# A four-layer attention stack: float32 keys and queries in layer 0, maxima moved ahead of the first eight-head phase, and an end in parts

## Chip, cores and metric

The kernel runs on one core of a Trainium2 chip, as one program written instruction by instruction for each engine, with semaphores between them. The metric is the device time of one execution in microseconds; the value quoted is the median of several runs. TensorE is PE below, VectorE is DVE, ScalarE is ACT, GpSimd is POOL, and SP is the engine that here only issues DMA transfers.

## What is computed

The input x has 4 images of 256 channels by 1024 positions, all in float32. Four self-attention layers follow each other:

```
layer 0: q = Wq x + bq (32 rows), k = Wk x + bk (32 rows), v = Wv x + bv (256 rows)
         out = gamma * (v softmax(q'k)') + x, then a batch norm over all images
layer 1: group norm, q, k, v of 256 rows, one head, output projection, x + out
layer 2: group norm (xn), eight heads of 32 rows, output projection, xn + out
layer 3: group norm, eight heads of 32 rows, output projection, x + out
```

## The kernel before

**Precision.** Most products use a fast 32-bit format of PE that keeps fewer bits. Where the full precision matters an operand is split into a high part (the value rounded to the fast format) and a low part (the rest, rounded again), and three products are added: high x high, low x high, high x low. A plain float32 matmul is also possible; the trace shows each as two records.

**Layers 0 and 1** (`one_head`) go image by image, b = 0 to 3. An image has eight tiles i of 128 queries. For each tile PE makes the scores of 128 x 1024 in one of the two slots of psD, DVE takes the row maximum, ACT the exponential, POOL multiplies by the inverse sum, PE transposes into psA, ACT and DVE split the result into PTH and PTL, and PE weighs the values into psO. The list `order` says which unit (scores "s", keys and queries "k", values "v") gets the next slot; a unit may have its slot only when the unit two places ahead has been taken. In layer 0 `project` makes keys and queries together, 64 rows: 12 matmuls from WH, WL, XH and XL. ACT writes the high part into KL (`high`), DVE the low part into QL (`low`), and SP copies them with six transfers (L736) into the stacks KH and QH of 96 rows, which the scores read with one product. All of this for the next image stands at tile 5 of the current one. At the start w0 is loaded, then image 0, then the constants; DVE splits w0 into WH and WL, ACT and DVE split X.

**Layers 2 and 3** (`eight_heads`) are one stream of 16 phases, for each a group of four heads of one image. A phase has 64 steps: half h, tile j and head q. A step is one score matmul (L1031, 97 rows: 96 of the stacks KS and QS and one that subtracts the maximum) and one exponential (L1209) into PR, which has room for four tiles j. POOL adds the tiles up into PA, `ADDS` = 5 additions a half (L1250); the weighted sum is on PE (`weigh`, L927), and `sums` (L939) adds PA and the last two tiles over the partitions. Between the steps stand side units, placed by hand by step number and made in four banks of psD in turn: "k", "q" and "K", "Q" (keys and queries of this group and of the next, six matmuls each half), "v" values, "m" and "a" (one maximum each of 128 x 512 scores, L1000 on PE and L1082 on DVE, for half 0 and half 1), "T" and "t" (the transposes that make the row of maxima, MROW), "z" (`sums`), and "p" (one 128 x 512 block of the output projection and its residual, L1073). "t" also carries the group means, on which POOL's factors and then ACT's normalised input (`XN_AT`, step 31) wait. Twelve (`EARLY`) of the 32 maxima for half 1 stand at the end of the phase before, the other 20 in the phase itself.

Ahead of phase 0 stands a fill (`phase(None, ...)`, place 0) with only side units. Its keys and queries are rounded on ACT, POOL makes the low parts (`low`, L1234), and SP copies them into the stack (24 transfers, L1281 and L1283). Then come 32 "m" and 12 "a" with "T" between, and "K", "Q" of group 1 behind the first maxima; ACT may take K only when the stack of group 0 has landed, since it overwrites SL. SP issues stack(0), stack(1) and then the row of maxima, L1288:

```python
FIRST_AT = {"k": (0.1, 0.2), "q": (0.3, 0.4), "b": (1,), "K": (8, 10), "Q": (12, 14)}
...
stack(0)
stack(1)
maxima(0, 0)
```

The tail, after phase 15, holds the last two pieces of `weigh`, `sums` of the last half, DVE's scaling (`take_half`), four output blocks with residuals, and one transfer of the last image.

Of the kernel before, what the change touches and what calls it, by code (L numbers as in the profile page):

```python
# [5 lines left out]
ALU = mybir.AluOpType  # L6
# [32 lines left out]
def attention_stack(nc, x, w0, w1, w2, w3, wp1, wp2, wp3, wv1, par_d, ident_d, gmat_d, out):  # L39
    with ExitStack() as ctx:  # L40
# [90 lines left out]
        def single_heads():  # L131

            with ExitStack() as stage:
# [14 lines left out]
                GBV = sb("GBV", [PART, CT], F32, stage)  # L148
                BNF = sb("BNF", [PART, CT, 2], F32, stage)
# [13 lines left out]

                s_const, s_memset = sem("constants_loaded"), sem("memsets_done")
# [5 lines left out]
                def one_head(layer):  # L170
# [43 lines left out]
                    with nc.Block() as block:  # L214
                        @block.tensor
                        def _(e):
# [9 lines left out]

                            def project(i, b):
                                if i == 0:
# [4 lines left out]
                                width = PART if L1 else 2 * K0  # L233
                                cols = slice(PART * i, PART * i + width)
                                for k, (ww, xx) in enumerate(((WH, XH), (WL, XH), (WH, XL))):
                                    if i == 0 and k == 2:
                                        e.wait_ge(xl_done, CT * (b + 1))
                                    for h in range(2):
                                        mv = slice(h * HALF, (h + 1) * HALF)
                                        for t in range(CT):  # L240
                                            mm = e.matmul(psD[0:width, slot, mv], ww[:, t, cols], xx[:, t, mv],
# [87 lines left out]
                            for b in range(B):  # L329
                                more = b + 1 < B  # L330
                                for i in range(NT):
# [3 lines left out]
                                    if not L1 and i == 5 and more:  # L335
# [24 lines left out]
                        def _(e):  # L360
# [145 lines left out]
                            for b in range(B):  # L506
                                more = b + 1 < B
                                for i in range(NT):
# [23 lines left out]
                                    if more and i == 5:  # L532
# [13 lines left out]
                        def _(e):  # L546
# [63 lines left out]
                            for b in range(B):  # L610
                                more = b + 1 < B
                                for i in range(NT):
# [8 lines left out]
                                    if more and i == 5:  # L621
# [11 lines left out]
                        def _(e):  # L633
# [7 lines left out]
                            def shift(b):  # L641
                                for t in range(CT):
# [123 lines left out]
        FIRST_AT = {"k": (0.1, 0.2), "q": (0.3, 0.4), "b": (1,), "K": (8, 10), "Q": (12, 14)}  # L766
        W3_AT = 28
        BANKS = 4
        SCORE_BANKS = 3

        def side_units(g, first=False, last=False):

            early, late = (0 if last else EARLY), (0 if first and g == 0 else 2 * ROWS - EARLY)
            tiles = ([("late", a) for a in range(2 * ROWS - late, 2 * ROWS)]
                     + [("first", a) for a in range(0 if last else 2 * ROWS)] + [("late", a) for a in range(early)])
# [3 lines left out]
            else:  # L779
                halves, step = dict({} if last else SIDE_AT[g]), STEPS / (4 * ROWS)  # L780
# [4 lines left out]
            units = [(u, at, i) for u, at_halves in halves.items() for i, at in enumerate(at_halves)]  # L785
            if first and g:
                units = [x for x in units if x[0] != "z" or x[2] == 0]
            for (kind, a), at in zip(tiles, ats):
                units.append(("a" if kind == "late" else "m", at, a))
                if a == 2 * ROWS - 1:  # L790
                    units.append(("t" if kind == "late" else "T", at + (LAG + 0.01) * step, 0))
# [25 lines left out]
        assert all(x[0] in "amtTzp" for u in UNITS[:4] for x in u[-BANKS:])  # L817
# [51 lines left out]
        def eight_heads_in(stage):  # L869
# [43 lines left out]
            with nc.Block() as block:  # L913
                @block.tensor
                def _(e):
# [15 lines left out]
                    def sums(full, P, h):  # L931

                        for j in (NT, *range(NT - DIRECT, NT)):
                            if j == NT:
                                wait(e, sum_done, ADDS * (2 * P + h + 1))
# [7 lines left out]
                            elif j < NT - 1:  # L943
# [22 lines left out]
                    def unit(place, r, k, P, p, G, g, norm, layers):  # L966
# [28 lines left out]
                        elif u in "am":  # L995
                            q, tile, h = i // NT, i // 2 % (NT // 2), i % 2
                            group = p if u == "a" and place and i >= EARLY else g
                            if u == "m" and i % NT == 0:
                                stacks_filled(e, G, [q])
                            mm = e.matmul(full, QS[0:STACK, group, int(u == "a"), q, tile * PART:(tile + 1) * PART],  # L1000
# [375 lines left out]
```

## Time and profile before

| what | us |
|---|---|
| median of 3 runs (lowest to highest) | 1654.55 (1653.58 to 1658.74) |
| the profiled execution's own time | 1656.73 |
| its span | 1654.8 |
| PE busy | 1542.6 (93%) |
| DVE, ACT, POOL busy | 1036.7, 866.1, 988.2 |
| first scores of layer 0 | 22.86 |
| first score of phase 0 | 581.86 |

The span is cut where the work changes: layers 0 and 1 up to 521 us, the fill up to 581.7, the 16 phases of some 65 us each up to 1628.6, and the tail. Times in the rows are microseconds from the start of the span; a busy share says how long an engine had work in flight, not that it was at its peak.

### The profile page before, as it was taken

The numbers are of one execution on the slowest core, as the hardware profiler recorded it, in microseconds if no ns is written. First come the engines' busy times: TensorE is split into PE (matmuls) and PEld (weight loads), VectorE is DVE, ScalarE is ACT, GpSimd is POOL, SyncE is SP. The second block draws the span as 40 slices with busy tenths as digits, with TensorE's granted clock in tenths as the row PEclk, the third lists the DMA queues.
The fourth block names the chain that finished last, engine by engine and source line by source line (L and its number), as shares of the span: only waits on it lengthen the run. The fifth ranks groups of instructions, "written<-read, shape, count | busy, mean of one in ns | idle before, by whom it ended". The sixth has DMA issues, their size and how long they took to land.

```text
span 1654.8 us, 21821 instructions
## 1 busy us (share of the span) xinstructions
PE 1542.6 (93%) x8238; PEld 993.2 (60%) x8238; DVE 1036.7 (63%) x1652; ACT 866.1 (52%) x1441; POOL 988.2 (60%) x392
## 2 busy tenths in 40 slices
PE   3888879999997789999999999999999999999986
PEld 2777757888886455555555555455555555555532
DVE  3556554544542666776776777677777777677741
ACT  3444324433433156657657567556665664765752
POOL 1212121221214168798698798967878879779874
PEclk7999989999999699999999999999999999999998
DMA  4000000000000501230330321303303123033000
GB/s 164 20 20 1 20 1 0 1 1 0 20 1 21 137 10 25 53 77 1 77 77 2 77 49 49 77 1 77 74 5 77 42 62 77 7 96 78 27 1 25
DMA packets 31720, 67.46 MB, mean 41 GB/s; under 512 B 7488, under 2 KB 9600, under 8 KB 31616
## 3 DMA queue, kind: packets, MB, share of 16 engines
q1 hardware_dynamic: 31616, 66.08, 16.2%
q8 instruction: 65, 1.06, 0.3%
q14 instruction: 39, 0.32, 0.1%
HBM read 8.08 MB, written 4.19 MB: 7 GB/s over the span
## 4 chain that ended last, share of the span: by engine, by line
PE 53%; POOL 7%; DVE 3%; SPq 2%; ACT 1%; issue 1%; POOLq 0%; DMA 0%; DVEq 0%; ACTq 0%
PE psO L927 12%; PE psD L1000 11%; PE psD L89 11%; PE psA L1031 9%; POOL PA L1250 6%; PE psD L939 5%; PE psO L1031 4%; DVE BNS L1082 2%; SPq L1281 1%; ACT PR L1209 1%; SPq L1283 1%; POOL SL L1234 1%; DVE sums_turned L1061 0%; DMA QS<-SL 0%; POOLq L913 0%
## 5 line engine op out<-in xcount | busy, mean ns | idle before, releaser
L1082 DVE TENSOR_REDUCE BNS<-psD 128x1 f32<-128x512 f32 x1024 | 638.0, 682 | 225.8 <-PE psD L1000 225.7
L1250 POOL TENSOR_TENSOR PA<-PA,PR 128x2048 f32<-128x2048 f32 x128 | 587.3, 4589 | 34.1 <-ACT PR L1209 18.9
L1209 ACT ACTIVATE PR<-psA 128x512 f32<-128x512 f32 x688 | 392.2, 604 | 242.5 <-PE psA L1031 218.2
L1000 PE MATMUL psD<-KS,QS 96*128 96x512 f32 x1024 | 417.2, 413 | 21.3 <-DMA QS<-SL 10.7
L1031 PE MATMUL psA<-QS,KS 97*128 97x512 f32 x688 | 290.9, 425 | 3.9 <-DMA QS<-MROW 2.2
L1209 ACT ACTIVATE PR<-psO 128x512 f32<-128x512 f32 x336 | 202.4, 602 | 160.2 <-PE psO L1031 160.2
L650 POOL TENSOR_SCALAR P<-P,RS 128x1024 f32<-128x1024 f32 x64 | 71.7, 1122 | 347.5 <-DVE RS L389 347.5
L927 PE MATMUL psO<-PR,V 128*32 128x512 f32 x2048 | 249.5, 605 | 7.5 <-DVE A L1067 5.6
L1000 PEld LDWEIGHTS psD<-KS,QS 96*128 96x128 f32 x1024 | 198.6, 194 | 76.1 <-DVE BNS L1082 17.8
L1250 POOL TENSOR_TENSOR PA<-PR 128x2048 f32<-128x2048 f32 x32 | 146.8, 4587 | 119.0 <-ACT PR L1209 119.0
L1031 PEld LDWEIGHTS psA<-QS,KS 97*128 97x128 f32 x688 | 130.9, 191 | 113.1 <-issue 57.9
L1031 PE MATMUL psO<-QS,KS 97*128 97x512 f32 x336 | 146.9, 437 | 0.7 <-ACT PR L1209 0.7
L927 PEld LDWEIGHTS psO<-PR,V 128*32 128x32 f32 x2048 | 53.6, 110 | 130.8 <-issue 82.4
L596 ACT ACTIVATE PTH<-psA 128x1024 fp32r<-128x1024 f32 x64 | 65.5, 1024 | 108.8 <-PE psA L279 108.8
L589 ACT ACTIVATE P<-psD,NM 128x1024 f32<-128x1024 f32 x64 | 71.2, 1112 | 95.3 <-DVE NM L382 95.3
L382 DVE TENSOR_REDUCE NM<-psD 128x1 f32<-128x1024 f32 x64 | 77.6, 1214 | 65.6 <-PE psD L89 65.5
L1031 PEld LDWEIGHTS psO<-QS,KS 97*128 97x128 f32 x336 | 63.7, 190 | 83.7 <-issue 46.5
L294 PE MATMUL psO<-PTH,VH 128*128 128x512 f32 x256 | 106.5, 416 | 4.4 <-issue 3.2
L395 DVE TENSOR_TENSOR PTL<-psA,PTH 128x1024 fp32r<-128x1024 f32 x64 | 78.2, 1222 | 39.7 <-ACT PTH L596 39.5
L294 PE MATMUL psO<-PTL,VH 128*128 128x512 f32 x256 | 102.2, 399 | 0.0
L294 PE MATMUL psO<-PTH,VL 128*128 128x512 f32 x256 | 102.2, 399 | 0.0
L1234 POOL TENSOR_TENSOR SL<-SL,SH 128x1024 fp32r<-128x1024 f32 x34 | 80.3, 2382 | 36.4 <-ACT SH L1159 36.4
(145 smaller groups left out, 1937.9 us busy)
## 6 DMA issues: line engine op xcount, KB each, us to landing
KS<-SH SPq DMA_DIRECT2D x128, 128.0 KB, 2.3
QS<-SH SPq DMA_DIRECT2D x128, 128.0 KB, 2.4
KS<-SL SPq DMA_DIRECT2D x64, 128.0 KB, 2.4
QS<-SL SPq DMA_DIRECT2D x64, 128.0 KB, 2.4
X<-x SPq DMA_DIRECT2D x4, 1024.0 KB, 7.5
out<-X SPq DMA_DIRECT2D x4, 1024.0 KB, 4.3
XN<-w SPq DMA_DIRECT2D x2, 768.0 KB, 8.0
KH<-KL SPq DMA_DIRECT2D x8, 128.0 KB, 2.3
```

The source lines that it names most:

```text
L89: last = e.matmul(out_ap, w, m, start=(i == 0), stop=(i == len(terms) - 1))
L294: mm = e.matmul(psO[:, t, :], vv[:, s, cols], pp[:, h, s, :], start=(s == k == 0), stop=(s == NT - 1 and k == 2))
L382: e.tensor_reduce(NM[:, g % 4:g % 4 + 1], psD[:, index[u] % 2, :], AX.X, ALU.max, negate=True).then_inc(max_done, 1)
L395: e.tensor_tensor(PTL[:, i // 4, :, cols], psT.rearrange("p (s t) -> p s t", s=NT), PTH[:, i // 4, :, cols].bitcast(F32), ALU.subtract).th ...
L927: mm = e.matmul(psO[cols, 0, :], V[:, j, PART * p + CH * q:PART * p + CH * q + CH], source[:, q, :], start=(j == 0), stop=(j == NT - 1))
L939: mm = e.matmul(full[CH * q:CH * q + CH, :], ones[:, 0:CH], source[:, q, :], start=(j == NT), stop=(j == NT - 1))
L1000: mm = e.matmul(full, QS[0:STACK, group, int(u == "a"), q, tile * PART:(tile + 1) * PART], KS[0:STACK, group, q, h * HALF:(h + 1) * HALF], ...
L1031: e.matmul(score_bank(s, p), KS[0:STACK + 1, p, q, j * PART:(j + 1) * PART], QS[0:STACK + 1, p, h, q, :], start=True, stop=True).then_inc( ...
L1082: top = e.tensor_reduce(MXH[:, h, q, tile:tile + 1], full, AX.X, ALU.max)
L1209: e.activation(PR[:, J % 4, (s % QUADH) * HALF:(s % QUADH + 1) * HALF], score_bank(s, p), ACT.Exp, scale=scale).then_inc(exp_done, 1)
L1234: e.tensor_tensor(SL[:, which, :].bitcast(F32R), SL[:, which, :], SH[:, which, :], ALU.subtract).then_inc(low_done, 1)
L1250: e.tensor_tensor(PA[:, :], PR[:, (J - 1) % 4, :] if j == 1 else PA[:, :], PR[:, J % 4, :], ALU.add).then_inc(sum_done, 1)
```

## The change

Layer 0: a tile WKQ gets the 64 columns of w0 for keys and queries by a transfer of its own, ahead of image 0 and w0; `project_narrow` multiplies it with X in plain float32 (two matmuls for each half of the positions); the projection of the next image with its `high` and `low` stands at tile 1 instead of 5; the values now wait for the split parts; POOL's `shift` of X waits until the projection has read X.

Eight heads: the fill makes only the 32 "m"; the 12 "a" move into phase 0, which so has 76 maxima over its 64 steps; K and Q of group 1 stand behind 23 maxima; DVE makes the low parts of group 0; SP sends the row ahead of stack(1). ("e" is the new name of the early maxima.)

End: in the last half POOL makes three additions, and `sums` reads PA and four tiles; the two output blocks of half 0 stand at steps 44 and 48 of the last phase and are stored from there; the other two stay in the tail, each with a transfer of its own.

```diff
+                wkq_loaded = sem("wkq_loaded")
...
-                            if i == 5 and b + 1 < B:
+                            if i == (5 if L1 else 1) and b + 1 < B:
                                 order += [("k", k, b + 1) for k in range(min(2, NQK))]
...
+                            def project_narrow(b):
+                                if b == 0:
+                                    e.wait_ge(wkq_loaded, 16)
+                                e.wait_ge(x_loaded[b], 16)
+                                slot = slot_taken(("k", 0, b))
+                                for h in range(2):
+                                    mv = slice(h * HALF, (h + 1) * HALF)
+                                    mm = split_products(e, psD[0:2 * K0, slot, mv],
+                                                        [(WKQ[:, t, :], X[:, b, t, mv]) for t in range(CT)])
+                                mm.then_inc(unit_full, 1)
...
                             def values(i, b):
                                 slot = slot_taken(("v", i, b))
+                                if not L1 and i == 0:
+                                    if b == 0:
+                                        e.wait_ge(w_low[layer], 1)
+                                    e.wait_ge(xh_done, CT * (b + 1))
+                                    e.wait_ge(xl_done, CT * (b + 1))
...
-                                    if not L1 and i == 5 and more:
+                                    if not L1 and i == 1 and more:
                                         project(0, b + 1)
...
-                                    if more and i == 5:
+                                    if more and i == (5 if L1 else 1):
                                         for k in range(min(2, NQK)):
                                             low(k, b + 1)
...
-                                    if more and i == 5:
+                                    if more and i == (5 if L1 else 1):
                                         for k in range(min(2, NQK)):
                                             high(k, b + 1)
...
                             def shift(b):
+                                e.wait_ge(unit_full, index["k", 0, b] + 1)
...
+                            e.dma_start(WKQ[:, :, :], w_dram[0][:, :, 0:2 * K0]).then_inc(wkq_loaded, 16)
+                            e.dma_start(X[:, 0], x_v[:, 0]).then_inc(x_loaded[0], 16)
                             e.dma_start(raw(0), w_dram[0]).then_inc(w_loaded[0], 16)
-                            e.dma_start(X[:, 0], x_v[:, 0]).then_inc(x_loaded[0], 16)
...
-        FIRST_AT = {"k": (0.1, 0.2), "q": (0.3, 0.4), "b": (1,), "K": (8, 10), "Q": (12, 14)}
+        FIRST_AT = {"k": (0.1, 0.2), "q": (0.3, 0.4), "b": (1,), "K": (28.1, 30.1), "Q": (32.1, 34.1)}
+        LAST_AT = {"p": (43.5, 47.5)}
+        LAST_ADDS = NT - 5
...
-            early, late = (0 if last else EARLY), (0 if first and g == 0 else 2 * ROWS - EARLY)
+            early = 0 if last or first and g == 0 else EARLY
+            late = 0 if first and g == 0 else 2 * ROWS if first else 2 * ROWS - EARLY
...
-                halves, step = dict({} if last else SIDE_AT[g]), STEPS / (4 * ROWS)
+                halves, step = dict(LAST_AT if last else SIDE_AT[g]), STEPS / max(len(tiles), 4 * ROWS)
...
-                        for j in (NT, *range(NT - DIRECT, NT)):
+                        for j in (NT, *range(adds + 1, NT)):
...
-                            mm = output(full, i, 2 * P, layers[3])
+                            mm = output(full, i, 2 * P + (G is None), layers[3])
...
-                        sums(bank(4, AFTER), NGRP - 1, 1).then_inc(d_full, 1)
-                        for i in range(2 * CT):
-                            e.wait_ge(vec_free, TAIL["vector"] + AFTER + i - BANKS + 2)
-                            output(bank(4, AFTER + 1 + i), i, 2 * NGRP, 3).then_inc(d_full, 1)
+                        sums(bank(4, AFTER), NGRP - 1, 1, LAST_ADDS).then_inc(d_full, 1)
+                        for c in range(CT):
+                            e.wait_ge(vec_free, TAIL["vector"] + AFTER + c - BANKS + 2)
+                            output(bank(4, AFTER + 1 + c), 2 * c + 1, 2 * NGRP, 3).then_inc(d_full, 1)
...
+                        if P is None:
+                            events += [(5, which, 0, "low") for which in range(2)]
+                        for _, which, k, what in sorted(events):
+                            if what == "low":
+                                e.wait_ge(high_done, which + 1)
+                                e.tensor_tensor(SL[:, which, :].bitcast(F32R), SL[:, which, :], SH[:, which, :],
+                                                ALU.subtract).then_inc(low_done, 1)
...
-                            for which in range(4):
-                                low(which // 2, which % 2)
+                            for which in range(2):
+                                low(1, which)
...
-                            for j in range(1, ADDS + 1):
+                            for j in range(1, (LAST_ADDS if G is None and h else ADDS) + 1):
...
                     stack(0)
+                    maxima(0, 0)
                     stack(1)
-                    maxima(0, 0)
...
-                    e.wait_ge(vec_free, TAIL["vector"] + AFTER + 1 + 2 * CT)
-                    e.dma_start(out_v[:, B - 1], X[:, B - 1]).then_inc(s_out, 16)
-                    e.wait_ge(s_out, 16 * B)
+                    e.wait_ge(vec_free, units_taken(NGRP, "p"))
+                    e.dma_start(out_v[:, B - 1, :, 0:HALF], X[:, B - 1, :, 0:HALF]).then_inc(s_out, 16)
+                    for c in range(CT):
+                        e.wait_ge(vec_free, TAIL["vector"] + AFTER + 2 + c)
+                        e.dma_start(out_v[:, B - 1, c, HALF:N], X[:, B - 1, c, HALF:N]).then_inc(s_out, 16)
+                    e.wait_ge(s_out, 16 * (B + CT))
```

## Rows read from the trace of the kernel before

**Rows 1.** The page: the chain that ended last, shares by engine.

```profile
PE 53%; POOL 7%; DVE 3%; SPq 2%; ACT 1%; issue 1%; POOLq 0%; DMA 0%; DVEq 0%; ACTq 0%
```

**Rows 2.** Stretches: busy time (instructions) per engine, PE's granted clock, DMA share, GB/s.

```profile
core 0: us, PE busy (x) PEld busy (x) DVE busy (x) ACT busy (x) POOL busy (x), PEclk, DMA share, GB/s
66.00:72.00 6.00, 4.00 (x15) 3.47 (x16) 1.39 (x2) 1.87 (x3) 0.37 (x1) 0.72 0.20 46
547.00:553.00 6.00, 0.37 (x2) 0.00 (x0) 0.00 (x0) 0.25 (x1) 0.00 (x0) 0.73 0.75 173
566.00:574.00 8.00, 7.84 (x15) 3.64 (x14) 7.93 (x15) 0.00 (x0) 0.00 (x0) 0.50 0.82 190
845.00:910.00 65.00, 64.87 (x365) 37.97 (x363) 46.26 (x80) 40.95 (x71) 55.90 (x25) 1.00 0.22 50
```

**Rows 3.** Timeline of the start: start, duration, engine, line, idle before and its releaser.

```profile
7.23 0.23 DVE L493 TENSOR_SCALAR GBV<-PAR 128x2 f32<-128x2 f32 x1 [2.05 <-DMA group_mean<-gmat]
10.16 1.94 PE L241 MATMUL psD<-XH,WH 128*64 128x512 f32 x4 [10.16 <-ACT XH L557]
14.84 1.11 ACT L576 ACTIVATE KL<-psD,PAR 64x1024 fp32r<-64x1024 f32 x1 [4.82 <-PE psD L241]
```

**Rows 4.** The chain: start, duration; one output block in a steady phase.

```profile
726.92 1.72 PE psD L89 x4
```

**Rows 5.** Timeline, images 1 to 2 of layer 0: tile 5 to the new scores.

```profile
108.75 1.14 PE L241 MATMUL psD<-XH,WH 128*64 128x512 f32 x4 [0.84 <-ACT XH L557]
...
111.26 1.21 DVE L395 TENSOR_TENSOR PTL<-psA,PTH 128x1024 fp32r<-128x1024 f32 x1
...
114.33 1.03 PE L279 MATMUL psA<-identity,P 128*128 128x128 f32 x8
...
120.49 0.70 PE L89 MATMUL psD<-KH,QH 96*128 96x512 f32 x2 [2.38 <-DMA QH<-QL]
```

**Rows 6.** Timeline: transposes of tile 2 in image 0, of tile 1 in image 1.

```profile
36.89 1.94 PE L279 MATMUL psA<-identity,P 128*128 128x128 f32 x8 [1.61 <-DVE PTL L395]
```

```profile
80.98 1.07 PE L279 MATMUL psA<-identity,P 128*128 128x128 f32 x8 [1.98 <-DVE PTL L395]
```

**Rows 7.** The chain through the fill ahead of phase 0.

```profile
550.30 2.34 DMA QS<-SL
...
557.46 1.38 PE psD L89 x6
...
559.12 13.25 DVE BNS L1082 x22
...
579.82 1.90 DMA QS<-MROW
```

**Rows 8.** Timeline: the first maximum of the fill.

```profile
540.99 1.19 PE L1000 MATMUL psD<-KS,QS 96*128 96x512 f32 x2 [10.70 <-DMA QS<-SL]
```

**Rows 9.** Groups by shape: count, busy us, mean ns of a subtraction of 128x1024.

```profile
L1234 POOL TENSOR_TENSOR SL<-SL,SH 128x1024 fp32r<-128x1024 f32 x34 | 80.3, 2382 | 36.4 <-ACT SH L1159 36.4
...
L427 DVE TENSOR_TENSOR XL<-X,XH 128x1024 fp32r<-128x1024 f32 x8 | 9.4, 1222 | 4.8 <-ACT XH L557 4.8
```

**Rows 10.** Timeline: ACT at step 31 of phase 0.

```profile
617.51 0.60 ACT L1209 ACTIVATE PR<-psA 128x512 f32<-128x512 f32 x1 [3.00 <-POOL SC L129]
```

**Rows 11.** The chain: a weighing of sixteen records, then the tail.

```profile
1571.37 1.85 PE psO L927 x16
...
1627.99 4.54 POOLq L913
...
1632.66 5.38 PE psD L939 x24
```

**Rows 12.** Timeline: the second residual of the tail.

```profile
1646.19 0.75 DVE L1073 SCALAR_TENSOR_TENSOR X<-psD,PAR,X 128x512 f32<-128x512 f32 x1 [2.04 <-PE psD L89]
```

**Rows 13.** The page: DMA issues, KB each, median us to landing.

```profile
out<-X SPq DMA_DIRECT2D x4, 1024.0 KB, 4.3
...
WP<-wp SPq DMA_DIRECT2D x2, 256.0 KB, 2.9
```

More of the change, by code:

```diff
@@ L148, in single_heads @@
                 GBV = sb("GBV", [PART, CT], F32, stage)
+                WKQ = sb("WKQ", [PART, CT, 2 * K0], F32, stage)
                 BNF = sb("BNF", [PART, CT, 2], F32, stage)
@@ L771, in side_units @@
         def side_units(g, first=False, last=False):
-            early, late = (0 if last else EARLY), (0 if first and g == 0 else 2 * ROWS - EARLY)
-            tiles = ([("late", a) for a in range(2 * ROWS - late, 2 * ROWS)]
-                     + [("first", a) for a in range(0 if last else 2 * ROWS)] + [("late", a) for a in range(early)])
+            early = 0 if last or first and g == 0 else EARLY
+            late = 0 if first and g == 0 else 2 * ROWS if first else 2 * ROWS - EARLY
+            tiles = ([("a", a) for a in range(2 * ROWS - late, 2 * ROWS)]
+                     + [("m", a) for a in range(0 if last else 2 * ROWS)] + [("e", a) for a in range(early)])
             if first and g == 0:
@@ L784, in side_units @@
                 ats = [(i + 0.5) * step - 1 for i in range(len(tiles))]
-            units = [(u, at, i) for u, at_halves in halves.items() for i, at in enumerate(at_halves)]
+            units = [(u, at, 2 * i if last and u == "p" else i) for u, at_halves in halves.items() for i, at in enumerate(at_halves)]
             if first and g:
@@ L788, in side_units @@
             for (kind, a), at in zip(tiles, ats):
-                units.append(("a" if kind == "late" else "m", at, a))
+                units.append((kind, at, a))
                 if a == 2 * ROWS - 1:
-                    units.append(("t" if kind == "late" else "T", at + (LAG + 0.01) * step, 0))
+                    units.append(("t" if kind == "a" else "T", at + (LAG + 0.01) * step, 0))
             return sorted(units, key=lambda x: x[1])
@@ L816, in attention_stack @@
         assert LOOP["all"] % BANKS == 0
-        assert all(x[0] in "amtTzp" for u in UNITS[:4] for x in u[-BANKS:])
+        assert all(x[0] in "ametTzp" for u in UNITS[:4] for x in u[-BANKS:])
         def base_of(kind, place, r):
@@ L994, in unit @@
                                                         [(WP[layer][:, t, cols], par(f"bv{layer}", 2)[:, t:t + 1]) for t in range(CT)])
-                        elif u in "am":
+                        elif u in "ame":
                             q, tile, h = i // NT, i // 2 % (NT // 2), i % 2
-                            group = p if u == "a" and place and i >= EARLY else g
+                            group = p if u == "a" else g
                             if u == "m" and i % NT == 0:
                                 stacks_filled(e, G, [q])
-                            mm = e.matmul(full, QS[0:STACK, group, int(u == "a"), q, tile * PART:(tile + 1) * PART],
+                            mm = e.matmul(full, QS[0:STACK, group, int(u in "ae"), q, tile * PART:(tile + 1) * PART],
                                           KS[0:STACK, group, q, h * HALF:(h + 1) * HALF], start=True, stop=True)
@@ L1101, in take @@
                         else:
-                            add_residual(i, proj, full, layers[3]).then_inc(vec_free, 1)
+                            add_residual(i, B - 1 if G is None else proj, full, layers[3]).then_inc(vec_free, 1)
                     def phase(P, p, G, g, place, r, layers, proj=None, norm=None, norm_b=None):
@@ L1124, in _ @@
                     take_half(bank(4, AFTER), 1, 1)
-                    for i in range(2 * CT):
-                        e.wait_ge(d_full, TAIL["all"] + AFTER + 2 + i)
-                        add_residual(i, B - 1, bank(4, AFTER + 1 + i), 3).then_inc(vec_free, 1)
+                    for c in range(CT):
+                        e.wait_ge(d_full, TAIL["all"] + AFTER + 2 + c)
+                        add_residual(2 * c + 1, B - 1, bank(4, AFTER + 1 + c), 3).then_inc(vec_free, 1)
                     e.drain()
```

21 lines of the change are left out of this document (11 added, 10 removed).

## The prediction

> **What bounds the kernel now.** I read the page first, then the stretches, then the timeline and the chain at the few places that the diff touches. The chain by engine [rows 1] puts 53% of the span on TensorE (PE) and 7% on GpSimd (POOL); the rest is thin. The stretches [rows 2] show that this average hides two kinds of time. In a steady phase of the eight-head layers (845 to 910 us) PE is busy without a gap at full clock, and the diff changes no instruction there, nor in layer 1. In the fill ahead of phase 0 (547 to 582 us), at the start, at the batch changes of layer 0 and in the tail, PE waits for something else, and its granted clock is partly or wholly at 0.50, the lower level of 1.2 GHz. Every edit sits in one of those places, so I cost them one at a time and let the rest shift as a block.
>
> **1. Start of layer 0.** Before, X is rounded on ACT and the first projection matmul goes at 10.16; the result is taken by ACT at 14.84 [rows 3]. After, PE multiplies X and WKQ as they come. It needs X and the constants, which DVE has at 7.23 [rows 3]. The price is that of float32 matmuls: an output unit of 512 columns (two matmuls, four records) takes 1.72 us at high clock [rows 4], twice that, 3.4, at half the clock. The narrow projection is four such matmuls: 3.4 us high, 6.9 low. The twelve old ones fill 10.16 to 14.8, 0.39 us each, where a batch later four take 1.14 (0.28 each, [rows 5]): this stretch runs low, so I take 6.8. 7.2 + 6.8 = 14.0 against 14.8, **-0.8 us**. Bounds: -4.2 (high clock) to 0. The split of W0 on DVE and XH, XL run beside it and are needed only for the values at tile 3; without that cover they would cost the 3 us that the old order paid. The small WKQ transfer stands ahead of X, w0 behind it; I cost both at nothing.
>
> The Trainium skill, "FP8 and Floating Point Precision", section "TensorE Precision Notes", counts true FP32 as four passes through the array, against three one-pass products in the old form, so it speaks against this edit in PE time. The rows agree: 2 x 1.72 = 3.4 us for the new projection against some 3 x 1.1 for the old. By the rule alone each projection would be a third dearer, by the rows about a tenth; the sum goes by the rows.
>
> **2. Batch changes in layer 0 (three).** Take batch 1 to 2 [rows 5]. The projection begins at 108.75 and fills PE for 3 us, the next transposes go at 114.33, and the first scores at 120.49, after PE stood 2.38 us for the last stack transfer. With projection, high and low part at tile 1, the transposes of tile 6 wait only for PTL of tile 5, done at 111.26 + 1.21 = 112.5: 1.7 us earlier. The weighing and the scores then follow with no wait: another 2.4 us. Together **-4.1 us each**, -12.3 for three; the first change also leaves 6 us at a mean clock of 0.72 [rows 2], worth 1.6. At tile 1 the work comes back. Batch 0: PE idles 1.61 us ahead of the transposes of tile 2 [rows 6], at low clock. A projection of 6.8 us, or about 5 if the clock rises during it, less that idle, with the high and low part behind it on ACT and DVE (queued behind them: the next maximum and PTL, for which the transposes wait): about +3. Batches 1 and 2: the 1.98 us of idle lies ahead of tile 1's transposes [rows 6], and the projection comes behind them, so it covers nothing; some of it at low clock makes it 4.9 us, of which 1.3 is won back because the weighing behind it finds the clock high: +3.6 each. Sum: -12.3 - 1.6 + 3 + 7.2 = -3.7, say **-3.5 us**. Bounds: -12 if all hides, +6 if all three cost 6.8 and the clock gives nothing.
>
> **3. Fill.** Before: K of group 1 stands behind two maxima, and ACT may take it only when the whole first stack has landed (550.30 + 2.34, [rows 7]), so PE works 0.4 of the 6 us from 547 to 553 [rows 2]; then DVE reduces at 13.25/22 = 0.602 us a tile [rows 7], 44 tiles in all; and the row goes out at 579.82, when SP has issued stack(1), and lands 1.90 us later [rows 7]. After:
> - Low parts on DVE: a pass of that size takes 1.22 us there against 2.38 on POOL [rows 9], so they end 2.2 us earlier, and so does all of the first stack.
> - SP issues a head's six transfers every 3.9 us. The first maximum, at 540.99 [rows 8], goes at 538.8. DVE then always has work: eight maxima take 4.9 us. It starts at 539.6, maximum 19 is done at 551.8, and K may be computed; the stack has landed at 550.5.
> - K, Q of group 1: four units of six matmuls, 1.38 us each at high clock [rows 7], up to twice that low; with two maxima between each, PE needs 9.1 us if the first runs low and the clock then rises, and DVE waits some. Maximum 31 is done at about 563.1, the row is made at 564.1, sent at once and lands in some 2 us: phase 0 begins at 566.5 instead of 581.86.
>
> That is **-15.4 us**. Bounds: -18 (K, Q at high clock), -12 (all at low clock). Stack(1) now follows the row on SP: 24 issues from 565.2, landed at 583, 17 us into phase 0; the maxima that read it come at step 27, some 30 us in, so 13 us cover it.
>
> **4. Phase 0** gets twelve more maxima of 0.24 us spacing on PE, 2.8 us. Its 32 maxima of half 1 end at step 26, so their transpose goes at step 29, at about 613.3 in the old timing, behind step 28's weighing. The row lands at about 616.9, where the score of step 32 would want it at 614.4. But ACT stood until 617.51 for the factors anyway, 3.00 us [rows 10], because POOL's five additions end so late; of the late row 0.5 us shows. Queued behind that transpose on PE are the group means, and behind those POOL's factors and ACT's input; the means come just ahead of POOL. Some of the 2.8 hides where POOL leads. **+2 us**; bounds 0 and +4.
>
> **5. Tail.** Before, the last weighing ends at 1628.6; POOL's fifth addition, begun at 1627.99, is awaited to 1632.53; the sums take 5.38 us until 1638.04 [rows 11]; then the half is scaled, four output units and residuals follow, and a transfer of 1 MB closes at 1654.8. After: three additions, done two steps of 4.7 us earlier; the sums read PA and four tiles, forty records, at the pace of the high clock (1.85 us per sixteen, [rows 11]) 4.7 us, since PE comes without a gap. Two output units of 1.72 us are moved into steps 44 and 48, where PE has slack behind POOL's cadence; I let them delay the last weighing by 0.8. So sums end at 1629.4 + 4.7 = 1634.1. From there to the end of the second residual it took 8.9 us (1646.19 + 0.75 less 1638.04, [rows 12]): 1643.0. The last piece is 256 KB, 2.9 us in the row of that size instead of 4.3 [rows 13]. End 1645.9: **-8.9 us**. Bounds: -11 (no delay, high clock in the outputs) to -4 (sums at low clock, +4.7).
>
> **Sum**: -0.8 - 3.5 - 15.4 + 2.0 - 8.9 = -26.6 us. The profiled execution took 1656.73 us for its span of 1654.8, 2.2 us above the median of the three runs; it gives 1630.1, and off the median 1654.55 it gives **1628 us** (-1.6%).
>
> **Rivals.**
> - *High clock.* PE is fed with fewer gaps at the start, at tile 1 and in the fill, and the clock stays high there: -3.4 at the start, -3 in the fill, -4 in layer 0: 1618 us. Against it: at 566 to 574 us the clock was 0.50 although PE worked steadily between maxima [rows 2]. Chance 0.17. Beside it stands the Trainium skill, "TensorE: Matmul & The Clock Gate", section "What's actually happening": the throttled state is the default and activity releases it. By that rule denser work would bring this case; the trace so far shows both.
> - *Fill won, phase 0 loses.* Stack(1) or the row of half 1 comes late after all and phase 0 stretches; of -15.4 + 2 only about -2 stays: 1640 us. It needs 13 us of slack to be wrong, or DVE to fall behind, which is busy 46 of 65 us in a phase [rows 2] and gets 8 more. Chance 0.12.
> - *Tail does little*: the moved units delay exponentials and the sums run at low clock: -3 instead of -8.9: 1634 us. Chance 0.12.
> - *Slower.* The moved projection holds one of two score slots until DVE has the low part. If each time everything queues up in series (6.8 projection, 1.1 high, 1.3 low, 1.2 maximum, 1.1 exponential, 1.1 normalisation: 12.6 us) layer 0 loses 3 x 12.6 - 13.9 = 24 us and eats the rest, -22; from 14 us each the kernel is slower than no change can explain, 1660 us. Against it: score 4 and the exponential of tile 3 don't wait for it. Chance 0.02.
> - *Nothing*: the waits named are plainly on the chain, so no net effect has 0.01.
>
> The forecast itself (1622 to 1634) has 0.56. A measurement here tells 0.3%, 5 us, from no change. Cases below 1649.6 hold 0.97; within, 0.01; slower, 0.02. The range takes in the forecast, most of the high-clock case and the phase 0 case: 1617 to 1640.
>
> **What would show it.** No wait for the stack transfer at the batch changes, a gap at tile 1 instead; phase 0's first score at about 562 instead of 581.86, with what layer 0 gave; ACT still waiting for POOL's factors at step 31; two additions fewer in the tail, and sums of about 4.7 us right behind the last weighing. The prediction is wrong if DVE idles over 5 us within the fill's maxima, if phase 0 takes over 72 us, or if layer 0 ends later than before.

## Result and the profile after

The changed kernel took 1629.39 us (median of 4 runs, 1626.74 to 1632.45) against 1654.07 us for the kernel before on the same chip: a ratio of 0.9845 with a 95% interval of 0.9820 to 0.9871, about 25.7 us or 1.5% faster. The forecast was 1628. Its profiled execution was the slowest of the four, 1632.45 us with a span of 1630.7; it is 24.3 us below the profiled execution of before. Executions of one kernel differ by 5 to 11 us here, more than most of the parts below are worth; what the parts share is told apart in the traces.

The page after, the chain by engine. PE's share rose from 53 to 55% and POOL's fell from 7 to 5% [rows 1].

```profile
PE 55%; POOL 5%; DVE 3%; SPq 2%; ACT 1%; issue 1%; DMA 1%; DVEq 0%; ACTq 0%; POOLq 0%
```

**The start.** Timeline of the changed kernel, to be read beside [rows 3].

```profile
6.64 1.28 ACT L576 ACT_TABLE_LOAD   x1 [6.64 <-DMA X<-x]
...
8.02 5.04 PE L89 MATMUL psD<-X,WKQ 128*64 128x512 f32 x8 [8.02 <-DMA group_mean<-gmat]
...
13.09 1.11 ACT L595 ACTIVATE KL<-psD,PAR 64x1024 fp32r<-64x1024 f32 x1 [3.09 <-PE psD L89]
...
18.73 0.60 SPq L757 DMA_DIRECT2D QH<-QL  x1
...
21.96 2.08 PE L89 MATMUL psD<-KH,QH 96*128 96x512 f32 x4 [8.90 <-DMA QH<-QL]
```

PE waits for the constants, the last of the small transfers, which now land 0.8 us later than the 7.23 of [rows 3]. The eight records take 5.04 us, between the two prices of the prediction (the weight loads of the first records are 0.85 us apart, those of the last 0.43). ACT has the result 1.75 us earlier than before, but the last stack transfer, issued at 18.73, is read only at 21.96, 3.2 us later, where each was 2.3 us on the page before; with the first scores at 22.86 before, 0.9 us is left.

**A batch change and what the projection costs at tile 1.** Timeline of the changed kernel: images 0 to 1, then tile 1 of image 1.

```profile
66.27 0.63 PE L89 MATMUL psD<-KH,QH 96*128 96x512 f32 x2
```

```profile
77.99 1.06 PE L298 MATMUL psA<-identity,P 128*128 128x128 f32 x8 [1.99 <-DVE PTL L414]
...
78.98 5.34 PE L89 MATMUL psD<-X,WKQ 128*64 128x512 f32 x8
...
84.37 1.11 ACT L595 ACTIVATE KL<-psD,PAR 64x1024 fp32r<-64x1024 f32 x1 [3.15 <-PE psD L89]
...
85.51 1.27 DVE L386 SCALAR_TENSOR_TENSOR QL<-psD,PAR,KL 64x1024 fp32r<-64x1024 f32 x1 [4.14 <-ACT KL L595]
...
87.58 1.04 PE L298 MATMUL psA<-identity,P 128*128 128x128 f32 x8
```

No scores wait for a transfer any more ([rows 5] had 2.38 us). But transposes to transposes now take 9.6 us (77.99 to 87.58) at tile 1, where they took 5.7 before (80.98 to 86.70): the wait of 1.99 us still stands ahead of the projection [rows 6], and the projection behind it. At the end of the image 4.3 us are won (1.7 behind tile 5 and 2.6 behind tile 6), so an image is only 0.4 us shorter.

**The fill.** The chain of the changed kernel, to be read beside [rows 7].

```profile
529.90 2.34 DVE SL L1138 x2
...
535.51 2.35 DMA QS<-SL
537.86 0.14 issue
537.99 13.10 PE psD L1024 x23
551.10 2.67 PE psD L89 x6
553.77 0.47 PE psD L1024 x2
554.24 1.38 PE psD L89 x6
...
562.52 1.81 DMA QS<-MROW
564.33 0.14 issue
564.46 0.76 PE psA L1055
```

This is the order that the prediction laid out: 23 maxima without a break from 538.0, the first K unit at low clock (2.67 us), the next at 1.38, and the row sent when it is made. Phase 0 starts at 564.46 instead of 581.86. Counted from the last residual of layer 1 (521.59 before, 520.98 after) the fill shrank from 60.3 to 43.5 us.

**Phase 0.** Timeline and stretches of the changed kernel; the columns of the second are those of [rows 2]. The last line of the timeline is the first score of phase 1.

```profile
597.48 0.55 SPq L1318 DMA_DIRECT2D QS<-MROW  x1
...
600.88 0.60 ACT L1239 ACTIVATE PR<-psA 128x512 f32<-128x512 f32 x1 [2.74 <-POOL SC L129]
...
610.93 0.50 PE L1024 MATMUL psD<-KS,QS 96*128 96x512 f32 x1 [0.99 <-DVE BNS L1106]
...
612.22 3.28 PE L951 MATMUL psO<-PR,V 128*32 128x512 f32 x16
...
637.25 0.40 PE L1055 MATMUL psA<-QS,KS 97*128 97x512 f32 x1
```

```profile
606.00:612.00 6.00, 5.00 (x27) 2.17 (x19) 4.47 (x9) 5.14 (x9) 5.15 (x3) 0.97 0.00 1
612.00:618.00 6.00, 6.00 (x28) 2.61 (x27) 3.65 (x7) 2.32 (x5) 4.78 (x2) 0.75 0.00 0
```

The same mark in the kernel before:

```profile
649.64 0.40 PE L1031 MATMUL psA<-QS,KS 97*128 97x512 f32 x1
```

From its first score to the first score of phase 1, phase 0 takes 72.8 us (564.46 to 637.25) where it took 67.8 (581.86 to 649.64): 5.0 us more.

The row of half 1 leaves at 597.48, 33.0 us into the phase. ACT's exponential of step 31 comes 36.4 us in; before it came 617.51 - 581.86 = 35.7 us in [rows 10]. These 0.8 us are about what the forecast gave the late row (0.5), but they are not the row: the exponential waits for POOL's factors, which POOL begins when its additions end, 33.7 us into the phase instead of 32.9. PE stands 1.13 us for the row, hidden behind that wait of ACT. The larger part of the loss, 4.2 us, comes in the second half, from step 32's exponential to the first of phase 1. A weighing of 16 records there runs at low clock, 3.28 us instead of 1.85 [rows 11].

The same place in the kernel with POOL's low parts (below), which has the same code from phase 0 on:

```profile
610.94 0.50 PE L1024 MATMUL psD<-KS,QS 96*128 96x512 f32 x1 [1.01 <-DVE BNS L1106]
...
611.97 1.92 PE L951 MATMUL psO<-PR,V 128*32 128x512 f32 x16
```

The same gap of 1.0 us, in which PE waits for DVE's maxima, but no low clock behind it. The nine traces with 76 maxima in phase 0 tell the two losses apart. In three of them the granted clock is 1.00 through the whole second half, which takes 33.7 us against 31.0 to 31.4 in the five with 64; in the other six it is 0.94 or 0.95 in the mean, and the half takes 34.8 to 37.9 us. So the maxima themselves cost about 2.5 us there (PE is busy 31.9 us instead of 30.3, the rest is waits), and the low clock, which the same code meets or misses, 1 to 4 us more.

**The tail.** Timeline of the changed kernel, to be read beside [rows 11, 12].

```profile
1614.03 1.07 PE L951 MATMUL psO<-PR,V 128*32 128x512 f32 x8 [0.20 <-ACT PR L1239]
1614.91 1.04 PE L963 MATMUL psD<-PA,ones 128*32 128x512 f32 x8
1615.77 3.62 PE L963 MATMUL psD<-PR,ones 128*32 128x512 f32 x32
1619.46 0.72 DVE L1085 STREAM_TRANSPOSE sums_turned<-psD 128x512 f32<-128x512 f32 x1 [15.28 <-PE psD L963]
...
1622.17 5.25 PE L89 MATMUL psD<-A,WP 128*128 128x512 f32 x8 [2.78 <-issue]
...
1627.46 0.75 DVE L1097 SCALAR_TENSOR_TENSOR X<-psD,PAR,X 128x512 f32<-128x512 f32 x1 [0.97 <-PE psD L89]
```

Forty records in 4.5 us, right behind the last weighing, where 24 took 5.38 us after a wait of 4 us. From the last weighing to the end it is 15.6 us instead of 26.2.

The ledger of the two profiled executions, from marks in the timelines:

| stretch | forecast | in the traces |
|---|---|---|
| start and layer 0 (last residual 231.37, then 229.28) | -4.3 | -2.1 |
| layer 1 | 0 | +1.5 |
| fill | -15.4 | -16.8 |
| phase 0 and the phases behind it (1046.75 us, then 1050.64) | +2.0 | +3.9 |
| tail | -8.9 | -10.6 |
| sum | -26.6 | -24.1 |

The fourth row lumps a loss of 5.0 us in phase 0 with 1.1 us won behind it, where the code is the same but for the last phase.

### The profile page after: what moved, and what is told of

Read it like the earlier page. It is cut to its first block, busy times and chain, and to the rows that moved or that the text cites. A ratio compares the mean times of both kernels' runs of the same rounds, so it can differ in the third digit from the quotient of the medians.

```text
span 1630.7 us, 21828 instructions
## 1 busy us (share of the span) xinstructions
PE 1541.4 (95%) x8238; PEld 990.5 (61%) x8238; DVE 1039.6 (64%) x1654; ACT 867.6 (53%) x1441; POOL 973.6 (60%) x388
## 4 chain that ended last, share of the span: by engine, by line
PE 55%; POOL 5%; DVE 3%; SPq 2%; ACT 1%; issue 1%; DMA 1%; DVEq 0%; ACTq 0%; POOLq 0%
PE psO L951 13%; PE psD L1024 13%; PE psD L89 11%; PE psA L1055 9%; PE psD L963 5%; PE psO L1055 5%; POOL PA L1280 4%; DVE BNS L1106 1%; SPq L1313 1%; SPq L1311 1%; POOL SL L1264 1%; DMA QS<-SL 1%; ACT PR L1239 0%; DVE sums_turned L1085 0%; DVE A L1089 0%
## 5 line engine op out<-in xcount | busy, mean ns | idle before, releaser
L1280 POOL TENSOR_TENSOR PA<-PA,PR 128x2048 f32<-128x2048 f32 x126 | 578.2, 4589 | 34.5 <-ACT PR L1239 19.9
L1264 POOL TENSOR_TENSOR SL<-SL,SH 128x1024 fp32r<-128x1024 f32 x32 | 75.7, 2384 | 42.2 <-ACT SH L1189 42.2
```

The costliest lines, as they stand in the source:

```text
L1264: e.tensor_tensor(SL[:, which, :].bitcast(F32R), SL[:, which, :], SH[:, which, :], ALU.subtract).then_inc(low_done, 1)
L1280: e.tensor_tensor(PA[:, :], PR[:, (J - 1) % 4, :] if j == 1 else PA[:, :], PR[:, J % 4, :], ALU.add).then_inc(sum_done, 1)
```

## Experiments

**One part at a time.** Each of the three parts was put alone on the kernel before. The parts are the diff shown above, cut by place.

> The kernel before with the layer 0 part alone. Theory A (the ledger of the two traces): the start gives 0.9 us, the three batch changes together about 1.2, and some of it is lost again in the clock of layer 1: 0.6 to 2.1 us faster than before, first score of phase 0 at 579.8 to 581.3. Theory B (the prediction): the part is worth 4.3 us, and the trace of the changed kernel shows less by the chance of its clock only: 1650 us, phase 0 at 577.6.

> The kernel before with the fill part alone. Theory A: the fill gives 16.8 us between the end of layer 1 and phase 0, phase 0 and the phases behind it give back about 3.9, so 13 us faster, 1641 us. Theory B (the prediction): -15.4 + 2 = -13.4; the two differ only in phase 0, which A has 5.5 us longer than before (first score to the row of maxima in its second half) and B 2 us longer.

> The kernel before with the end by parts alone. Theory A: 10 to 11 us faster (sums begun at once and at high clock, two output blocks fewer, small last transfer), 1643.5 us. Theory B: the gain depends on the high clock in the sums, which the trace had by chance: 4 to 6 us.

| kernel | median us | ratio to before, 95% interval |
|---|---|---|
| layer 0 part alone | 1650.58 | 0.9964 (0.9951 to 0.9978) |
| fill part alone | 1641.30 | 0.9914 (0.9900 to 0.9928) |
| end alone | 1644.50 | 0.9940 (0.9924 to 0.9956) |

In microseconds: -6.0, -14.2 and -9.9, with some 2.5 us either way. Their product is 0.982, at the lower edge of the interval of all together, so the parts add up only just within the measurement (-30.1 against -25.7). For layer 0 alone the two theories split: timed, 3.6 to 8.1 us, it excludes theory A's 0.6 to 2.1 and takes in theory B's 4.3, while its own trace, the longest of its executions, shows phase 0 at 581.30, theory A's number. The seven traces with the projection at tile 1 (the changed kernel and six experiments) tell more: layer 0's last residual stands at 228.1 to 229.5 us in five and at 223.2 and 223.5 in two, mean 227.4; the three with the old form have it at 230.4 to 231.4, mean 231.0. The mean is worth 3.7 us; the changed kernel's profile was one of the long ones. The two short ones had the higher clock: 0.90 from 20 to 70 us in one (0.78 in the changed kernel), 0.99 from 70 us on in the other (0.96). The fill alone: it takes 44.7 us from layer 1's last residual instead of 60.3, and phase 0 takes 74.2 us instead of 67.8, so theory A. The end alone: the sums run from the last weighing (1626.87) to 1631.23, 4.4 us, as in the changed kernel, so the high clock there was no chance.

**The place of the projection.** The changed kernel with one constant changed, 1 into 4 or 5.

```diff
-                            if i == (5 if L1 else 1) and b + 1 < B:
+                            if i == (5 if L1 else 4) and b + 1 < B:
...
-                                    if not L1 and i == 1 and more:
+                                    if not L1 and i == 4 and more:
```

> The changed kernel with layer 0's projection of the next image at tile 4 instead of tile 1. Theory A: at tile 1 the projection lies wholly on PE's path behind the transposes (3.6 to 5.3 us each time) and high and low part behind it, which eats the 4.1 us won at the batch change; behind the values and at tile 4, where PE waits for DVE's low parts of X, part of it hides: 3 to 6 us faster than the changed kernel, 1624 to 1626. Theory B: PE is the bound at every tile from image 1 on, so the place doesn't matter: within 1 us of the changed kernel.

> The changed kernel with layer 0's float32 projection at tile 5, its old place. Theory A (the place counts, not the form): the wait for the stack at the batch change is back, layer 0 ends at 229 to 231 us as before the change and with tile 1, against 221 with tile 4; 9 to 10 us slower than the tile 4 kernel, 0 to 2 slower than the changed one. Theory B (with tile 4 the gain came from not waiting for XH and XL any more): tile 5 keeps most of it, layer 0 ends at 223 to 225.

Tile 4: 1619.04 us median, ratio 0.9797 (0.9774 to 0.9819). Tile 5: 1630.21, ratio 0.9851 (0.9832 to 0.9869). Layer 0 ends at 220.92 with tile 4 and at 228.47 with tile 5. (Tile 4's profiled execution, 1629.68 us, was by far its longest; the other four took 1618.4 to 1622.5.) Timeline of the tile 4 kernel, tile 4 of image 1:

```profile
97.12 1.23 DVE L393 TENSOR_TENSOR VL<-psD,VH 128x1024 fp32r<-128x1024 f32 x1 [1.66 <-ACT VH L601]
...
98.50 3.62 PE L89 MATMUL psD<-X,WKQ 128*64 128x512 f32 x8 [1.13 <-DVE VL L393]
```

PE has caught up with DVE here: it waits 1.13 us until the low part of the values frees the slot, and DVE has a row of work to do (residual, statistics, maximum) while PE projects. The projection also runs at a granted clock of 1.00 and takes 3.62 us, in all three images and in all three kernels with tile 4; at tile 1 it took 4.27, 5.34 and 5.34 us in the changed kernel. How much of the gain is the cover by DVE's work and how much the clock, no run separates; at tile 5 it is 3.65 us too, and the gain is gone. From the transposes of tile 0 in one image to those in the next it is 48.2 us twice (70.39, 118.57, 166.77), against 50.9 and 52.5 in the changed kernel (71.72, 122.61, 175.13) and 49.7 and 51.3 with tile 5. So the place decides, and theory A holds with a larger size than it gave; two more kernels with tile 4 below end layer 0 at 220.74 and 219.44, and the shortest of the seven with tile 1 ends it 2.3 us behind the longest of these three. Tile 5 is too late for the stack (the new scores wait 1.52, 2.41 and 2.44 us for it at the three changes), tile 1 stands in PE's way.

**The twelve maxima back in the fill.**

```diff
-            early = 0 if last or first and g == 0 else EARLY
-            late = 0 if first and g == 0 else 2 * ROWS if first else 2 * ROWS - EARLY
+            early = 0 if last else EARLY
+            late = 0 if first and g == 0 else 2 * ROWS - EARLY
```

> The changed kernel with the twelve maxima of half 1 back in the fill (44 there, 64 in phase 0), all else as changed. Theory A (phase 0 pays 5 us for them: 2.8 of PE time, 0.8 for the late row, the rest a stretch at low clock): the fill is 12 x 0.60 = 7.2 us longer, phase 0 starts that much later and is 5 us shorter, 2 us slower in all. Theory B (the prediction's 2 us for phase 0): 5 us slower than the changed kernel.

It came out the other way: 1626.83 us, ratio 0.9819 (0.9802 to 0.9836), lower than the changed kernel's 0.9845 rather than above it. The two intervals overlap, so that it is faster is not shown; that it is 5 us slower, theory B, is excluded, and theory A's 2 us lie at the far edge. (One of its six executions took 8453 us; it is left out of the ratio, and nothing here explains it.) Both theories gave the fill 7.2 us for the twelve. Its timeline shows why that was wrong:

```profile
559.83 0.19 DVE L1110 TENSOR_REDUCE MX<-BNS 128x16 f32<-128x32 f32 x1
559.93 1.88 DVE L1106 TENSOR_REDUCE BNS<-psD 128x1 f32<-128x512 f32 x3
560.16 0.27 PE L1029 MATMUL psD<-identity,MX 128*16 128x128 f32 x1 [0.45 <-DVE MX L1110]
560.67 5.17 PE L1024 MATMUL psD<-KS,QS 96*128 96x512 f32 x9 [0.24 <-DVE BNS L1106]
561.73 0.27 DVE L1123 TENSOR_SCALAR MROW<-psD 16x128 fp32r<-16x128 f32 x1
561.92 5.45 DVE L1106 TENSOR_REDUCE BNS<-psD 128x1 f32<-128x512 f32 x9
562.02 0.56 SPq L1318 DMA_DIRECT2D QS<-MROW  x1
565.63 0.63 PE L1055 MATMUL psA<-QS,KS 97*128 97x512 f32 x1
```

Nine of the twelve run on PE while the row is made and on its way, which the 32-maxima fill spends idle. From the last residual of layer 1 to phase 0 it is 47.4 us against 43.5: the twelve cost 3.9 us, not 7.2. On the other side, phase 0 (first score to first score) takes 67.6 to 68.4 us in the five kernels with 64 units in it, mean 67.9; in the nine with 76 it takes 70.3 to 74.2, mean 72.4. Without the six that had a low clock in the second half it is 71.0. From phase 0's first score to the last weighing the means are 1045.4 and 1051.4 us, but 1.5 of these 6 us arise behind phase 0, where the two groups' times overlap (976.0 to 979.0 and 975.9 to 981.7). So moving the twelve out of the fill saves 3.9 us and costs 3.0 to 4.5 in phase 0: about even, within what these traces can tell.

**The order on SP, the low parts, and K.** Three single reversals of the fill part.

```diff
                     stack(0)
-                    maxima(0, 0)
                     stack(1)
+                    maxima(0, 0)
```

> The changed kernel with SP sending the row of maxima behind stack(1), as before. Theory A: with K and Q of group 1 now at the end of the fill, stack(1) is issued only from some 565 us and needs 15.8 us, so the row is sent at 581 and phase 0 begins at about 583, 18 us later: 1647 us, most of the fill's gain gone. Theory B: the row waited 4 us behind the stack before and costs the same now: 1633 us.

1646.64 us, ratio 0.9949 (0.9932 to 0.9965). Timeline of this kernel:

```profile
555.93 0.28 DVE L1123 TENSOR_SCALAR MROW<-psD 16x128 fp32r<-16x128 f32 x1 [0.45 <-PE psD L1029]
```

```profile
557.37 0.53 SPq L1311 DMA_DIRECT2D KS<-SH  x1
```

```profile
573.46 0.59 SPq L1318 DMA_DIRECT2D QS<-MROW  x1
575.47 0.77 PE L1055 MATMUL psA<-QS,KS 97*128 97x512 f32 x1 [19.57 <-DMA QS<-MROW]
```

The row is made at 556.2 and sent at 573.46. The fill is 61.9 us long, 18.4 more than in the changed kernel. Theory A, exactly: once K and Q stand at the end, the row must go first, or nothing of the fill's gain is left.

> The changed kernel with POOL making the low parts of group 0 again. Theory A: the stack begins 2.3 us later (2 x 2.38 instead of 2 x 1.22) and phase 0 with it: 2 us slower than changed. Theory B: DVE, not the stack, sets the fill's end, so it is hidden: no change, phase 0 at 564.5.

1631.23 us, ratio 0.9857 (0.9835 to 0.9879). Timed it can't be told from the changed kernel; in the trace the fill is 45.8 instead of 43.5 us, as theory A has it. Fills of the changed kernel's code were 43.5 to 45.2 us long in six traces, as the second K unit behind the maxima met a low clock or not, so that the fill's length alone would not carry this. But the first stack transfer is issued 13.6 us behind layer 1's last residual instead of 11.3, and the first maximum goes at 19.3 instead of 17.0 to 17.1, 2.3 us later than in every one of the six.

> The changed kernel with K and Q of group 1 at their old places, behind the first maxima of the fill. Theory A: PE and DVE stand from the fourth or so maximum until the whole first stack has landed and ACT may write SL again, phase 0 begins 6 to 9 us later: 1636 us. Theory B: the stack's landing by head bounds the maxima anyway, so it costs under 2 us.

1637.60 us, ratio 0.9894 (0.9873 to 0.9916); the fill is 52.7 us, 9.2 longer. Timeline of this kernel:

```profile
543.62 1.26 ACT L1200 ACTIVATE SL<-psD,PAR 128x512 f32<-128x512 f32 x2 [18.80 <-DMA QS<-SL]
544.37 1.22 PE L1024 MATMUL psD<-KS,QS 96*128 96x512 f32 x2 [6.06 <-ACT SL L1200]
```

PE stands 6.06 us behind K, which ACT may not take before the whole stack has landed. Theory A.

**Five additions in the last half.** `LAST_ADDS = ADDS`.

> The changed kernel with POOL making all five additions of the last half. Theory A: the sums wait for POOL again until 3.5 us later and run at low clock (5.4 us for 24 records against 4.5 for 40): 4 to 5 us slower than changed. Theory B: sixteen more records on PE cost what the wait gave: within 1 us.

1631.51 us, ratio 0.9862 (0.9842 to 0.9882). Timeline of this kernel:

```profile
1614.49 1.06 PE L951 MATMUL psO<-PR,V 128*32 128x512 f32 x8 [0.20 <-ACT PR L1239]
1618.76 1.94 PE L963 MATMUL psD<-PA,ones 128*32 128x512 f32 x8 [3.21 <-POOL PA L1280]
1620.42 2.81 PE L963 MATMUL psD<-PR,ones 128*32 128x512 f32 x16
```

From the last weighing to DVE's transpose it is 7.7 us against 4.4: 3.4 us by the trace, a little under what theory A gave; the timed difference (about 2.8) is inside the intervals.

**Towards the fastest version.** The tile 4 kernel with the twelve maxima in the fill, and the tile 4 kernel with phase 0's maxima of half 1 set closer:

```diff
                 ats = [(i + 0.5) * step - 1 for i in range(len(tiles))]
+                if first:
+                    rest = (STEPS - 2 * ROWS * 0.7) / (len(tiles) - 2 * ROWS)
+                    ats = [(i + 0.5) * 0.7 - 1 if i < 2 * ROWS else 2 * ROWS * 0.7 - 1 + (i - 2 * ROWS + 0.5) * rest
+                           for i in range(len(tiles))]
```

> Both findings together: projection at tile 4 and the twelve maxima of half 1 back in the fill. If the gains are independent (8 to 9 us for the place, 1 to 3 for the maxima) it is 1616 to 1619 us, the fastest version; if the clock takes one of them back it is no faster than the tile 4 kernel, 1619 to 1622.

> The tile 4 kernel with phase 0's 32 maxima of half 1 set 0.7 steps apart instead of 0.84, so that their transpose goes at step 24 instead of 29, and the other 44 spread over the rest. Theory A (most of phase 0's 5 us is PE time for twelve maxima more, which stays): at most 1 to 2 us faster than tile 4. Theory B (the late row and the gap that it leaves, with the low clock behind it, are the larger part): 3 to 5 us faster.

1622.97 us, ratio 0.9807 (0.9787 to 0.9826), and 1623.89 us, ratio 0.9809 (0.9789 to 0.9830), on another chip than tile 4's 0.9797. None of the three can be told from the others; the first lies 1 us above both of its ranges, and the second shows none of theory B's 3 to 5 us. In its trace tile4_back12 has what was hoped for: layer 0 ends at 220.74 and first score to last weighing takes 1045.95 us, the shortest span of all traces, 1621.0 (tile 4's own trace is its longest execution). Timed, it is not shown to beat tile 4 alone. With closer maxima the row of half 1 goes out 30.3 us into phase 0 instead of 33.1, and phase 0 takes 72.7 us against 72.9 with tile 4, both with a mean clock of 0.95 in the second half: the late row costs next to nothing. All three tile 4 kernels beat the kernel before; tile 4 alone also lies, barely, outside the changed kernel's interval of 0.9820 to 0.9871, the other two overlap it at its lower edge, so that they beat it is likely and not shown.

## Why the prediction was right, and where its terms were off

The forecast of 1628 us with -26.6 as its sum met 1629.39 and -25.7 by the ratio. The mechanisms showed in the traces, but that the sum came within 1.4 us is in part luck: the fill and the tail gave 3.1 us more than forecast, and layer 0, layer 1 and the phases took 5.6 us back in the profiled pair. One of its own signs of being wrong came true: phase 0 took 72.8 us, over the 72 that it named. The other two did not (DVE idled 3.1 us within the fill's maxima, and layer 0 ended earlier than before). Step by step:

1. **Start (-0.8).** Right in size, 0.9 in the trace. The parts were off both ways: PE began 0.8 us later than assumed, since the constants now come behind w0; the matmuls took 5.0 instead of 6.8 us, since only the first of them ran at half pace; and the stack transfers were slower, beside the input loads that now lie later (that these loads are the reason is argued from their place, not tried). "I cost both at nothing" missed that.
2. **Batch changes (-3.5).** The two sides of the sum, 4.1 us won at each change and some 3.6 paid at tile 1, showed as argued: 4.3 won with no wait for the transfer, and 3.9 paid at tile 1. With the start, layer 0 gave 2.1 us in the profiled pair and 3.7 in the mean over ten traces, for 4.3 forecast. The bound "-12 if all hides" was the interesting end: at tile 4 another 7 us (219.4 to 220.9 against a mean of 227.4) were to be had. The high-clock rival met part of this, not its total: low-clock records remain, such as the weighing of 3.28 us at a granted clock of 0.75. The Trainium skill ("TensorE: Matmul & The Clock Gate", section "What's actually happening") has activity release the clock; the trace agrees for the fill, where the second K unit takes 1.38 us after a first of 2.67, and at the end, where the sums run at 0.11 us a record once they follow the weighing without a gap. That PE has work in flight is not enough to tell the clock: from 612 to 618 us it was busy throughout at a mean of 0.75.
3. **Fill (-15.4).** Right, 16.8 us; three of its parts were confirmed by their reversal: K's place (9.2 us), the row's place on SP (18.4 us when taken back alone), the low parts (2.3 us). They overlap and don't add. The fourth, twelve maxima fewer, was worth 3.9 us.
4. **Phase 0 (+2.0).** This term was mis-sized, and outside its bounds of 0 and +4 in the pair and in the mean: phase 0 took 5.0 us more in the profiled pair and 4.5 in the mean, 3.0 of them where the second half kept its clock. "Some of the 2.8 hides where POOL leads" did not hold, and of the late row, priced at 0.5, nothing shows: POOL's factors, not the row, held ACT at step 31, and sending the row 2.8 us earlier changed nothing. What the sum left out is the low clock in the second half, in six of nine traces, worth 1 to 4 us. In the profiled run it comes behind PE's wait of 0.99 us for DVE's maxima; since the same wait stands in a trace without it, the wait alone does not bring it, and what does stays open. The fill-won, phase-0-loses rival had the direction but asked for 13 us.
5. **Tail (-8.9).** 10.6 in the trace, 9.9 timed alone. The last weighing was not delayed by the moved blocks (from phase 0's first score it comes after 1044.3 us both with the end alone and with layer 0 alone), and from the last residual to the end it was 2.5 us.

Not seen at all was that keeping the twelve maxima in the fill was half free, since nine of them run while the row is made and sent. The prediction took the whole shift as a gain because it counted phase 0's start and not what stood between the row's making and its landing. The slower rival, everything in series behind the projection, did not come: tile 1 took 9.6 us from transposes to transposes instead of 5.7, not 12.6 us more.

## What to carry over

When work is moved out of a serial stretch, look for the wait that it used to fill: here a transfer in flight hid nearly half of it, and moving it to a stretch where PE is the bound cost about as much as it saved. When work is moved earlier to hide a transfer, move it to where its engine already waits for another, not merely early enough: tiles 1 and 4 both hide the transfer, and they are 7 us apart in the mean. A row that frees the next phase must be issued ahead of everything on its queue that isn't needed yet.

## What was not expected of the hardware

The clock dips make the size of a small edit a matter of many traces. Nearly identical code (the spacing of some maxima differs in one of the nine, the end in two) from phase 0's first score to the last weighing took 1047.2 to 1054.7 us, and identical layer 0 code 223.2 to 229.5 us; layer 1, from layer 0's last residual to its own, took either 290.0 to 290.4 or 291.7 us and nothing between, at a mean granted clock of 0.98 and 0.97. The same instructions after the same wait of 1.0 us met a low clock in one trace and not in another. The float32 projection of eight records took 4.3, 5.0 and 5.3 us at three places of one execution, and 3.62 us where the clock was full.
